# Second attention of a four-batch block: small tail operations spread around the row maxima, and an inverse deviation in Newton steps on GpSimd

## What is computed

```python
x = conv_block(x)                      # 1x1 convolutions, softmax over 1024 positions, residual, ReLU
t = to_tokens(x)                       # (4, 1024, 256)
...
qkv = layernorm(t) @ w_qkv             # 8 heads of 32
attn = softmax(q @ k.T * scale)        # (4, 8, 1024, 1024)
t = t + (attn @ v) @ w_out + b_out
...
flat = layernorm(t)                    # eps 1e-5
logits = flat @ Wr                     # 8 experts
top_vals, top_idx = top_k(logits, 2)
top_w = softmax(top_vals)
for e in range(8):                     # gates are zero but for the two chosen experts
    y = gelu(flat @ W1[e] + b1[e]) @ W2[e] + b2[e]
    out = out + gates[:, e:e + 1] * y
t = t + out
```

## Time and profile before

| | us |
|---|---|
| three runs | 1194.0, 1190.9, 1186.65 |
| median | 1190.9 |
| profiled execution | 1189.1 |
| its span in the trace | 1187.3 |
| PE busy | 1107.1 (93%) |
| DVE busy | 816.8 (69%) |
| ACT busy | 635.2 (54%) |
| POOL busy | 583.1 (49%) |

### The profile page before, as it was taken

How to read it: one execution, slowest core, us unless ns; L and a number is a source line. 1 busy time by engine, 2 the same in 40 slices (tenths; PEclk the granted TensorE clock), 3 DMA queues, 4 the chain that set the end, 5 groups by cost and what they waited for, 6 DMA issues and landing times.

```text
span 1187.3 us, 28583 instructions
## 1 busy us (share of the span) xinstructions
PE 1107.1 (93%) x10376; PEld 732.0 (62%) x10376; DVE 816.8 (69%) x1495; ACT 635.2 (54%) x1151; POOL 583.1 (49%) x461
## 2 busy tenths in 40 slices
PE   7999999979999999999999998699999999999985
PEld 4454645434444544454445444599899989989874
DVE  4666566766788787788778882678655655655783
ACT  3566676556677667756775675343333333333332
POOL 3424242314888751774277437247555444543530
PEclk9999999998999999999999999899999999999998
DMA  5355842626123321432243214724333233323328
GB/s 173 89 178 208 315 159 96 184 66 195 51 56 87 90 74 31 121 101 76 61 121 90 56 47 103 299 33 81 52 55 55 43 51 55 49 45 44 47 37 288
DMA packets 98885, 120.61 MB, mean 102 GB/s; under 512 B 29024, under 2 KB 76064, under 8 KB 98112
## 3 DMA queue, kind: packets, MB, share of 16 engines
q1 hardware_dynamic: 75280, 70.40, 20.2%
q0 software_dynamic: 20400, 42.08, 16.0%
q10 hardware_dynamic: 3072, 6.30, 1.5%
HBM read 73.10 MB, written 45.47 MB: 100 GB/s over the span
## 4 chain that ended last, share of the span: by engine, by line
PE 78%; DVE 7%; ACT 4%; issue 4%; DMA 3%; DVEq 3%; POOL 1%; SPq 1%; ACTq 0%; POOLq 0%
PE PP L987 23%; PE PP L1406 13%; PE PP L1296 9%; PE PP L1270 9%; PE PP L1158 4%; PE PP L1086 3%; PE PP L1218 3%; PE PP L1280 3%; PE PP L1003 3%; PE PP L1285 3%; PE PP L1118 1%; DVE mxp L1693 1%; PE PP L1366 1%; DMA WORK<-v_d 1%; DMA res_d<-WORK,lb 1%
## 5 line engine op out<-in xcount | busy, mean ns | idle before, releaser
L917 ACT ACTIVATE WB<-PP 128x512 f32<-128x512 f32 x512 | 268.1, 605 | 138.2 <-PE PP L1296 138.1
L1693 DVE TENSOR_REDUCE mxp<-PP 128x2 f32<-128x1024 f32 x242 | 285.0, 1219 | 60.9 <-PE PP L1218 59.3
L961 ACT ACTIVATE WORK<-PP,b1c 128x256 f32<-128x256 f32 (+1 forms) x320 | 140.2, 450 | 246.2 <-PE PP L987 203.4
L690 POOL TENSOR_TENSOR WB<-WB 128x1024 f32<-128x1024 f32 x80 | 188.7, 2361 | 58.9 <-PE PP L1285 56.9
L746 POOL DMA_INDIRECT res_d<-WORK,lb x70 | 118.7, 1696 | 169.5 <-DVE WORK L1927 147.9
L1406 PE MATMUL PP<-WB,WORK 128*128 x1704 | 192.9, 273 | 0.6 <-DVE WORK L1910 0.6
L987 PE MATMUL PP<-WORK,WB 128*128 128x256 f16 (+1 forms) x1552 | 178.7, 276 | 10.4 <-DVE WORK L1896 10.4
L1406 PEld LDWEIGHTS PP<-WB,WORK 128*128 128x128 f16 x1704 | 164.8, 98 | 19.9 <-issue 0.9
L987 PEld LDWEIGHTS PP<-WORK,WB 128*128 (+1 forms) x1552 | 154.6, 103 | 30.2 <-issue 11.7
L987 PE MATMUL PP<-WORK 128*128 128x128 f16 (+6 forms) x1086 | 159.8, 299 | 13.2 <-DVE WORK L1896 4.3
L1296 PE MATMUL PP<-WORK 97*128 97x256 f16 x1024 | 158.5, 277 | 8.9 <-ACT WB L917 7.5
(11 more groups left out here) (306 smaller groups left out, 1196.5 us busy)
## 6 DMA issues: line engine op xcount, KB each, us to landing
WORK<-in_L_ffn_W_dram POOLq DMA_DIRECT2D x32, 512.0 KB, 4.3
res_d<-WORK SPq DMA_DIRECT2D x8, 1024.0 KB, 4.5
late_d<-WB POOLq DMA_DIRECT2D x1, 6144.0 KB, 19.2
WB<-late_d ACTq DMA_DIRECT2D x3, 2048.0 KB, 15.2
v_d<-WORK SPq DMA_DIRECT2D x4, 1024.0 KB, 4.8
WORK<-q_hi_d SPq DMA_DIRECT2D x16, 256.0 KB, 3.7
WORK<-v_d SPq DMA_DIRECT2D x8, 512.0 KB, 5.7
WORK<-k_hi_d SPq DMA_DIRECT2D x16, 256.0 KB, 3.7
```

The lines of the kernel that those rows point to most:

```text
L690: pool.tensor_tensor(PS[n % 2], PR[n % 3][:, 0], PR[n % 3][:, 1], ALU.add).then_inc(s("pair_kept"), 1)
L917: act.activation(PR[n % 3][:, c // 2, c % 2 * 2:c % 2 * 2 + 2], SCORES[m % 3] .rearrange("p (h n) -> p h n", h=2), ACT.Exp).then_inc(s("e_ ...
L961: act.activation(hid[:, k, 0:width], hidden_bank(k)[:, 0:width], ACT.Gelu, bias=b1c[:, bass.ds(e, 1), k], scale=1.0 / WSCALE)\
L1693: dve.tensor_reduce(mxp[:, n // 4 % 2, i, h:h + 2, k], PP[2 + h // 2][:, :].rearrange("p (h n) -> p h n", h=2), X_AXIS, ALU.max).then_inc( ...
```

## The change

The five parts of the top-2 choice become twelve, and the places, gates and the early table are cut up in the same way: a part is one operation or a few independent ones. A place in the program is now a pair (step, 0), (step, 1) or (step, 2): before the step's first reduction, between the two, or after the second. A counting semaphore `tail_kept` takes the place of most drains: each small operation adds one, and a later part waits for the count. `join_halves`, the release of the row (`row_kept`) and the statistics move to the start of a step. ACT's square root leaves the loop; the variance's bits are shifted on DVE (`tail_guess`), and POOL makes the inverse deviation in three Newton steps of 128x8 operations (`tail_rstd`, step 14). `DIRECT` loses steps 13 and 16 to 20. The last batch's tail, after the attention, takes the same parts in a row and keeps the square root. Three semaphores around indirect DMAs become one (`dma_on`).

```diff
-VAR_AT, SD_AT, RSTD_AT = 13, 14, 15
 NORM_AT, HIGH_AT = (16, 17, 19, 20, 22, 23, 25, 26), (18, 21, 24, 27)
-PICK_AT, RANK_AT, PLACE_AT = (13, 14, 15, 16, 17), 18, (18, 19, 20)
-GEXP_AT, GATE_AT = 18, 20
+AGGREGATE_AT, RSTD_AT, RANK_AT, GEXP_AT = (13, 0), 14, 18, 18
+PICK_AT = ((12, 2), (13, 2), (14, 0), (14, 1), (14, 2), (15, 0), (15, 1), (15, 2), (16, 0), (16, 1), (16, 2), (17, 0))
+PLACE_AT = ((19, 0), (19, 1), (19, 2), (20, 0))
+GATE_AT = ((20, 0), (20, 1), (20, 2))
...
-DIRECT = tuple(range(13, 29))
+DIRECT = (14, 15) + tuple(range(21, 29))
...
+            def tail_rstd(n):
+
+                pool.wait_ge(s("stat1_kept"), n)
+                var, est = small[:, 1], small[:, 5]
+                pool.tensor_scalar(small[:, 6], var, -0.5, None, ALU.mult)
+                pool.drain()
+                pool.tensor_scalar(est.bitcast(I32), est.bitcast(I32), -1, GUESS, ALU.mult, ALU.add)
+                for last in (False, False, True):
+                    pool.drain()
+                    pool.tensor_tensor(small[:, 7], est, est, ALU.mult)
+                    pool.drain()
+                    pool.tensor_tensor(small[:, 7], small[:, 7], small[:, 6], ALU.mult)
+                    pool.drain()
+                    pool.tensor_scalar(small[:, 7], small[:, 7], 1.5, None, ALU.add)
+                    pool.drain()
+                    pool.tensor_tensor(small[:, 3] if last else est, est, small[:, 7], ALU.mult)
+                pool.tensor_scalar(small[:, 0], mv[:, :, 0], -1.0, None, ALU.mult)
+                pool.drain()
+                pool.tensor_tensor(small[:, 4], small[:, 0], small[:, 3], ALU.mult).then_inc(s("rstd_kept"), 1)
...
             for n in range(B * STEPS):
                 b, t = n // STEPS, n % STEPS
+                if b and t == RSTD_AT:
+                    tail_rstd(b)
                 if not direct(n):
                     add_pair(n)
...
-                    if t == SD_AT:
-                        tail_deviations(b)
...
-            def join_halves(u):
-
-                dve.drain()
+            def join_halves(u, b):
+
+                dve.wait_ge(s("mx_kept"), b * 2 * STEPS + 8 * (u + 1))
...
-                dve.drain()
+
+            def row_kept(before, at):
+
+                dve.wait_ge(s("c_kept"), before + at)
                 dve.sem_inc(s("nmr_kept"), 1)
...
+            def last_kept():
+
+                dve.wait_ge(s("tail_kept"), done[0])
+
+            def keeps(op):
+
+                op.then_inc(s("tail_kept"), 1)
+                done[0] += 1
...
+                elif part == 10:
+                    keeps(dve.tensor_tensor(oh2, weight, per_tile(rs[:, 3]), ALU.is_equal))
                 else:
-                    dve.tensor_tensor(pick16[:, :, :], oh1, oh2, ALU.add)
-                    dve.tensor_tensor(rs[:, 2], rs[:, 2], small[:, 3], ALU.mult)
-                    dve.drain()
-                    dve.sem_inc(s("pick_kept"), 1)
+                    keeps(dve.tensor_tensor(pick16[:, :, :], oh1, oh2, ALU.add))
+                    dve.wait_ge(s("rstd_kept"), n)
+                    last_kept()
+                    dve.tensor_tensor(rs[:, 2], rs[:, 2], small[:, 3], ALU.mult).then_inc(s("pick_kept"), 1)
...
+                    if not first:
+                        if t in STATS_AT:
+                            tail_statistics(STATS_AT.index(t))
+                        tail_part((t, 0))
+                    for m in groups:
+                        reduce_heads(m, b, 0)
+                    if not first:
+                        tail_part((t, 1))
+                    for m in groups:
+                        reduce_heads(m, b, 2)
+                    if not first:
+                        tail_part((t, 2))
```

More of the change, by code:

```diff
@@ L1727, in tail_rstd, with tail_pick @@
                                          op0=ALU.mult, op1=ALU.mult).then_inc(s("rstd_kept"), 1)
[L1729 to L1731 removed]
+            def tail_pick(part, n, before):
+                last_kept()
+                weight = per_expert(w8[:, :], NT)
                 if part == 0:
[L1733 to L1735 removed]
+                    dve.wait_ge(s("c_kept"), before + slots[0])
+                    keeps(dve.tensor_reduce(rs[:, 0], logit, X_AXIS, ALU.max))
@@ L1780, in tail_places, with tail_gates @@
                     dve.tensor_copy(idx[:, :, :], rs[:, 0:2]).then_inc(s("idx_kept"), 1)
-            def tail_gates(tail, n):
+            def tail_gates(part, tail, n):
                 here = slice(tail * NT, (tail + 1) * NT)
[L1785 to L1793, removed]
+                last_kept()
+                if part == 0:
+                    dve.wait_ge(s("gexp_kept"), n)
+                    keeps(dve.tensor_scalar(rs[:, 3], rs[:, 2], 1.0, None, ALU.add))
+                elif part == 1:
+                    keeps(dve.reciprocal(rs[:, 4], rs[:, 3]))
+                else:
+                    keeps(dve.tensor_copy(meta[:, here, 0, 2].bitcast(F32), rs[:, 4]))
+                    last_kept()
+                    dve.tensor_tensor(meta[:, here, 1, 2].bitcast(F32), rs[:, 4], rs[:, 2], ALU.mult)\
+                       .then_inc(s("gate_kept"), 1)
@@ L1805, in early_table @@
                 elif part == 2:
[L1806 to L1809, removed]
+                    keeps(dve.tensor_reduce(full, over8.rearrange("p k e -> p e k"), X_AXIS, ALU.add))
                 elif part == 3:
-                    dve.tensor_tensor(cmp8, per_expert(incl, EARLY), per_tile(seq8), ALU.is_le)
@@ L1853, in attend, with tail_part @@
                 slots[0] = 0
+                row_at = None
+                def tail_part(at):
+                    if at in PICK_AT:
+                        tail_pick(PICK_AT.index(at), b, before)
+                    if at == AGGREGATE_AT:
+                        tail_aggregate()
+                    if at == (AGGREGATE_AT[0], 1):
+                        tail_variance()
+                    if at == (AGGREGATE_AT[0], 2):
+                        tail_guess()
+                    if at in PLACE_AT:
+                        tail_places(PLACE_AT.index(at), before, b)
+                    if at in GATE_AT:
+                        tail_gates(GATE_AT.index(at), b - 1, b)
+                    if last and at in EARLY_AT:
+                        early_table(EARLY_AT.index(at), before)
                 for t in range(STEPS):
                     n = b * STEPS + t
-                    for m in max_groups(t, first, last):
-                        reduce_group(m, b)
-                        if m % 4 == 3:
-                            join_halves(m // 4)
+                    groups = max_groups(t, first, last)
+                    if row_at is not None:
+                        row_kept(before, row_at)
+                        row_at = None
+                    joined = t + LEAD - 1
+                    if joined % 4 == 3 and joined >= MAX_EARLY and t and max_groups(t - 1, first, last):
+                        join_halves(joined // 4, b)
+                    if not first:
[10 more added lines that the diff above has]
+                        tail_part((t, 2))
                     u = row_unit(t, first, last)
@@ L2104, in _ @@
             deviations("stat1_kept")
-            for part in range(4):
-                tail_pick(part, B)
-                if part == 1:
+            for part in range(PICKS - 1):
+                tail_pick(part, B, before)
+                if part == 4:
                     keep_turned(0, 0)
             tail_rstd(B)
-            tail_pick(4, B)
-            for part in range(3):
+            tail_pick(PICKS - 1, B, before)
+            for part in range(PLACES_PARTS):
                 tail_places(part, before, B)
-            tail_gates(B - 1, B)
+            for part in range(len(GATE_AT)):
+                tail_gates(part, B - 1, B)
             def copy_first(t, e, part):
```

158 lines of the change are left out of this document (82 added, 76 removed).

## The result

The changed kernel takes 1195.69 us (median of 9 runs, 1193.11 to 1198.76) against 1190.44 for the kernel before (9 runs, 1186.33 to 1194.0): ratio 1.0047, 95% interval 1.0031 to 1.0063. It is slower by half a per cent. The forecast was 1188 (range 1171 to 1198), a little faster than before.

A forecast was written before the change was run, and what follows sets the result against it. PE was taken to bound the kernel (78% of the chain). From 1189.1 us, 19.6 saved at PE's pace, less 5.75 a batch for collisions and 1.5 for the clock, net -0.8: 1188 (range 1171 to 1198).

The forecast's parts named there:

- The table loads: Steps 14 and 15: square root off ACT removes two loads, 2.56 us of ACT a batch, and PE's 1.18 us wait.
- Direct steps: A direct step takes 3.33 us, 2.89 with POOL's addition; six fewer save 2.6 us a batch.
- The Newton chain: Sixteen POOL operations from step 14, 0.3 us each, 4.8 us, hidden by seven us of slack before step 17; no cost.
- rival C: Newton chain late for step 17 at 0.73 us an operation, 3.3 us a batch: 1198 us; chance 0.13.
- The collisions: Small two-input DVE operations in steps 14 to 22 wait for POOL's additions: 5.75 us a batch on 28.4.
- the clock: PE stands about 2 us in step 14 and its clock falls: 0.5 us a batch (bounds 0 and 1.3), +1.5.
- Steps 17 and 18 were to lose 1.3: Addition 16 meets second one-hot, choice L1813 and product (17, 0) ahead of step 17's reductions: +1.3 us, including step 18.
- Rival B: Collisions don't bite, small operations fall into gaps between additions: 29.2 us a batch, 1172 us; chance 0.27.
- the "products": Additions 18 and 19 meet the three products of (19, 1) between two reductions: +0.75 us (bounds 0 and 2.36).
- the terms for steps 19 to 22: Additions 18 and 19 at (19, 1): +0.75 us; addition 20 at (20, 2): +1.3; longer reduction loop: +0.4.
- step 20's loss: Addition 20, behind `tail_low` on POOL, meets the gates' product (20, 2): +1.3 us (bounds 0 and 2.36).
- The change touches these nine steps and little else.: Only steps 14 to 22 of batches 1 to 3, 104.88 us together, were to change; steps 23 to 31 keep their length.

The follow-up runs named there:

- changed kernel again: The changed kernel run once more with no edit, its second profiled execution, beside the kernel before: 1195.21 us, ratio 1.0039.
- first execution: First profiled execution of the changed kernel, no further edit: 1198.76 us, 3.1 above its median.

## Why the prediction was wrong

**What held.** The table loads went, and PE's wait for ACT with them. Direct steps are worth 0.44 us: step 19 takes 2.88 us with the addition (changed kernel again) and 3.32 without. The Newton chain is harmless: from 447.43 to 452.90, 5.5 us, 0.34 an operation with its drain, where 0.3 was taken; rival C needed 0.72. The collisions were priced at 5.75 us on 28.4, 34.2 us a batch without the clock. Batch 1 of the first execution, the one at full clock, took 33.95. The sizes can be set beside the version with no addition, with 0.44 added for each step that an addition shortens: steps 14 and 15 lose 8.17 - 6.99 + 0.44 = 1.62 us, where 2.0 was taken, and steps 16 to 22 lose 25.78 - 24.42 + 5 x 0.44 = 3.56, where 3.75 was. PE waits 2.28 us for the row's copy behind L1796, where before it had waited 0.26:

```profile
440.72 0.40 PE L1218 MATMUL PP<-WB 32*128 32x512 f16 x4 [0.26 <-DVE nmr L1707]
```

Steps 17 and 18 were to lose 1.3, and PE waits 1.02 and 0.48. Rival B fell with that: the small operations did not find the gaps. Not every place was right. L1813 and the gates' product L1854 kept 0.23 and 0.17 us, since the operation ahead of each had waited the addition out. Of the three operations of (19, 1), the "products", only the first stood, 0.57 us, and for a normalisation; the addition of step 19 held the cast of the indices, L1840. That the terms for steps 19 to 22 came out so near is in part luck.

The Trainium skill's rule in "SBUF — State Buffer", section "Who interferes with whom", agrees: of two that contend, the later waits until the other's whole instruction is over, and the reductions beside additions kept their 1.2 us each. The same section names copies, casts and `tensor_scalar` among the instructions that can contend too, when they run in a mode that uses both ports. L1852, a copy, L1840, a cast, and L1873, a `tensor_scalar`, stood with a single input; whether they ran in that mode no run shows. The prediction had spoken of operations with two inputs alone, and laid step 20's loss on the product behind the copy.

**The step that failed: the clock.** "I take 0.5 us a batch (bounds 0 and 1.3): +1.5." In the first execution steps 14 and 15 cost 9.63 in two batches and 8.17 in one: the lower clock (0.82 in the mean) is worth 1.46 us. In the second it came in all three batches. So the term is 2.9 us in the first execution and 4.4 in the second, not 1.5: 1.46 in each batch in which the clock falls, above the bound I had set. The rows of before held this size: in steps 14 and 15 PE is busy 7.78 us in batch 1 and 5.88 in batch 0, and only 0.44 of that difference is the direct step. I looked at one group of matmuls and took 0.5. The clock doesn't fall every time: it fell in five of six such batches of the changed kernel, where PE stands 2.28 us, in five of six of the kernel before, and in none of the three with the Newton steps alone, where PE stands 1.20. The term's error is 1.4 to 2.9 us of the loss.

**A second step: "The change touches these nine steps and little else."** The early table's parts, spread between reductions like the rest, meet the low half on POOL: 28.73 us for steps 23 to 30 of batch 3, 27.26 before and with the table late. That is 1.5 more. With both, the forecast of 0.8 us faster becomes 2.1 slower with the first execution's clock and 3.6 with the second's. The traces agree: from the start of batch 1 to the last step of batch 3 the two executions take 345.2 and 346.6 us, 343.0 in the first execution of before (341.5 in its second, where the clock stayed up in one batch).

The other 2 to 3 us of the 5.2 measured lie ahead of batch 0, in batch 0 or among the experts, where single profiles differ by more than that; they stay open. Little of it can lie in the last batch's changed tail: from the start of batch 3's last step to the experts' first second-layer product (L1406, now L1430) it is 41.2 and 40.6 us in the two executions of before, 41.2 and 41.3 after. Against the forecast of 1188 there is 1.3 us more, since the sum started from one execution of 1189.1 and the median of before is 1190.44.

## What to carry to other kernels

Before moving work to POOL, list what small DVE operations stand in the same microseconds, and what else is queued on POOL behind it: an operation that costs nothing itself can push its neighbours onto something that matters. Put such operations ahead of nothing that feeds the bounding engine. And where PE is to stand for some 2 us, price the lower clock behind it at what it costs in the trace of the same kernel over all the steps that it reaches, here 1.5 us, and not at what one group of matmuls loses.

## What the runs showed of the hardware that was not expected

- A single-input copy of 128x8 from SBUF to SBUF takes 0.17 us alone and 1.25 beside an addition on POOL, and a single-input cast of 128x16 (L1840) 0.17 and 0.92, while the statistics of 128x256, also single-input, were not slowed.
- L1873 was issued at 713.66, ahead of the recorded start of the low half at 714.27, and stood all the same; POOL was issuing an indirect DMA until then. In three other traces it was the two-input operation ahead of it, L1872, that was issued 0.65 us ahead of the low half and stood 1.85 us, to its end. Whether the DMA held them, or POOL's recorded start is late, was not tried.
- Counting on a semaphore is a little cheaper than a drain between dependent small operations: in the last batch's tail, undisturbed, such operations start 0.30 us apart before and 0.26 after.
